# A decoder layer on one core: five of eight batches normed, and four routed to their experts, amid the last three attention rounds

## What is computed

```python
x1 = mixer(x)                                  # gated cumulative sums, a layer norm, a projection; then post-norm
q, k, v = x1 @ Wq, ctx @ Wk, ctx @ Wv          # 16 heads of 16
sm = softmax(einsum('nlhd,nshd->nlhs', q, k) / 4, axis=1)     # over the 512 queries
attn = einsum('nlhs,nshd->nlhd', sm, v).reshape(N, L, 256)
x2 = layernorm(x1 + attn @ Wo + bo)
logits = x2 @ Wr + br                          # 8 experts
top_idx = top_k(logits, 2)                     # two experts a token, softmax over the two logits
y = sum over the two experts of weight * (relu(x2 @ W1[e] + b1[e]) @ W2[e] + b2[e])
out = layernorm(x2 + y)
```

## Time and profile before

| what | value |
|---|---|
| median of three runs | 2198.38 us (2195.28 to 2202.76) |
| the profiled execution | 2195.98 us, of which 2194.3 us are the span of the profile |
| busy in the span | PE 90%, DVE 80%, ACT 70%, POOL 34% |
| last copy of attention outputs starts at | 1528.13 us |
| first matrix product of the experts at | 1647.92 us |

### The profile page before, as it was taken

One profiled execution on the slowest core, in us unless ns is written; L12 is line 12 of the kernel. 1 busy time (PEld: TensorE's weight loads), 2 busy tenths in 40 slices (PEclk: granted clock), 3 DMA queues, 4 the chain that ended last, 5 costly groups with the idle time before them and its releaser, 6 DMA issues.

```text
span 2194.3 us, 43516 instructions
## 1 busy us (share of the span) xinstructions
PE 1981.7 (90%) x10630; PEld 1044.8 (48%) x10638; DVE 1754.2 (80%) x3559; ACT 1540.5 (70%) x4345; POOL 736.3 (34%) x983
## 2 busy tenths in 40 slices
PE   7898998899999999999999998888829999999994
PEld 3554555322322232222322221112729999999994
DVE  5889885799999999999999999998635555555554
ACT  4655565899999999999999999998402333233333
POOL 0112111244444444444444441111563333333333
PEclk9989999999999999999999999999859999999997
DMA  4111105776758576676668576661771222222225
GB/s 156 44 44 72 58 24 130 193 125 116 112 110 145 118 110 117 119 124 135 90 131 136 108 111 92 123 77 42 223 197 32 37 36 37 36 36 36 36 36 168
DMA packets 126117, 212.39 MB, mean 97 GB/s; under 512 B 31554, under 2 KB 94786, under 8 KB 124882
## 3 DMA queue, kind: packets, MB, share of 16 engines
q1 hardware_dynamic: 98272, 151.74, 37.8%
q0 software_dynamic: 26240, 59.00, 10.2%
q10 hardware_dynamic: 1554, 1.05, 0.2%
HBM read 138.38 MB, written 73.74 MB: 97 GB/s over the span
## 4 chain that ended last, share of the span: by engine, by line
PE 39%; ACT 30%; issue 18%; DVE 7%; POOL 3%; DMA 2%; ACTq 1%; DVEq 0%; SPq 0%; POOLq 0%
ACT w_all L1429 26%; PE psum L1715 12%; PE psum L1725 11%; PE psum L473 6%; DVE neg_max L1336 3%; POOL list_all L1595 3%; PE psum L1239 2%; PE psum L1271 2%; ACT w_all L822 1%; PE psum L1702 1%; DMA v_all<-w_all 1%; PE psum L500 1%; ACTq L1428 1%; DVE stats L1016 0%; DVE stats L1995 0%
## 5 line engine op out<-in xcount | busy, mean ns | idle before, releaser
L1429 ACT ACTIVATE w_all<-psum,neg_max 128x512 f32<-128x512 f32 (+1 forms) x1664 | 1111.1, 736 | 18.2 <-DVE neg_max L1336 16.6
L1336 DVE TENSOR_REDUCE neg_max<-psum 128x1 f32<-128x512 f32 (+1 forms) x1664 | 1024.9, 677 | 17.3 <-PE psum L1271 14.2
L1271 PE MATMUL psum<-qst,kst 96*128 96x512 bf16 (+1 forms) x1664 | 527.7, 389 | 73.1 <-ACT w_all L1429 63.1
L1239 PE MATMUL psum<-w_all 128*32 128x512 f32 (+1 forms) x3328 | 448.9, 612 | 9.5 <-DVE w_all L1350 9.3
L1271 PEld LDWEIGHTS psum<-qst,kst 96*128 96x128 bf16 (+1 forms) x1664 | 130.0, 98 | 658.1 <-ACT w_all L1429 639.0
L1769 ACT ACTIVATE hid<-psum,b 128x128 f32<-128x128 f32 x568 | 161.9, 368 | 393.1 <-PE psum L1715 393.1
L1429 ACT ACTIVATION_READ_ACCUMULATOR w_all<-psum,neg_max 128x1 f32 (+1 forms) x1664 | 426.8, 257 | 0.0
L1402 POOL TENSOR_TENSOR w_all<-vst,inv 128x64 f32<-128x64 f32 (+1 forms) x416 | 121.0, 291 | 658.3 <-DVE inv L1304 654.7
L1715 PE MATMUL psum<-xst,w 128*128 128x128 f32 x2272 | 267.4, 277 | 0.0
L1715 PEld LDWEIGHTS psum<-xst,w 128*128 128x128 f32 x2272 | 261.6, 193 | 0.1
L1725 PE MATMUL psum<-area,hid 128*128 128x256 f32 x1136 | 257.0, 380 | 0.0
(11 more groups left out here) (209 smaller groups left out, 1878.1 us busy)
## 6 DMA issues: line engine op xcount, KB each, us to landing
kst<-k_parts SPq DMA_DIRECT2D x384, 112.0 KB, 6.5
k_parts<-k_out POOLq DMA_DIRECT2D x52, 336.0 KB, 3.0
w_all<-in_W SPq DMA_DIRECT2D x16, 1024.0 KB, 11.9
area<-in_ctxT SPq DMA_DIRECT2D x16, 896.0 KB, 4.7
vst<-v_all SPq DMA_DIRECT2D x64, 224.0 KB, 9.2
qst<-q_parts SPq DMA_DIRECT2D x192, 64.0 KB, 5.9
v_all<-area POOLq DMA_DIRECT2D x13, 896.0 KB, 4.3
q_parts<-q_out POOLq DMA_DIRECT2D x24, 256.0 KB, 3.0
```

The costliest lines, as they stand in the source:

```text
L1239: last = pe.matmul(psum[j * PAD:(j + 1) * PAD, 6, :], v_scaled[0:r, pb, j, :], probs_at[pb][0:r, j, :], start=t == 0, stop=t == ST - 1)
L1271: pe.matmul(psum[0:r, 2 * sbuf + i, :], kst[:, h, j, t * P:t * P + r], qst[:, h, j, :], start=True, stop=True).then_inc(scores_ready, 1)
L1336: v.tensor_reduce(neg_max[0:r, sbuf, i:i + 1], psum[0:r, 2 * sbuf + i], AX_X, ALU.min) \
L1429: act.activation(probs_at[pb][0:r, j, :], psum[0:r, 2 * sbuf + i, :], ACT.Exp, bias=neg_max[0:r, sbuf, i:i + 1], scale=-1.0, accum_out=sum ...
```

## The change

`NORMED_AT = (6, 13, 37, 44, 68)` names five steps among the 78 tile steps of the last three rounds. From each of them one batch (0 to 4) begins its norm, at fixed offsets: sums on PE in bank 7 at +0, +1, +3, +4 (`SUM_AT`), DVE's adds at +1 and +4, its statistics at +2 and +5, ACT's logarithm and exponential at +6 and +7, the shift on DVE and the scaling at +8 and +9. The scaling (`scale_rows`) is done by POOL here and not by ACT. Batches 0 to 3 (`PLACED`) are also turned (+13, +15, with ACT's copies in the same steps), scored and chosen (+17 to +20), given slots (+26 or +22) and scattered, one transfer a step from +27 or +28. The steps for batches 5 to 7, and the route of 4 to 7, stay in the route stage after attention.

The last three rounds are written out on every engine, where before two of them were in a loop on PE and DVE, and all three on ACT and POOL. The small tiles move into `xwk`, which is free after the last filled round. `y2`, `x2t` and `x2` move from the experts' own buffer `w1` to the places of the last three blocks of `w1_all` (`LATE_W1 = 3`), so that these three blocks are loaded only after the last `x2` is stored and scored. `y2` has two halves now. The table load that ACT had ahead of the route stage (`preload_act_table_set`) is gone.

```diff
+    NORMED_AT = (6, 13, 37, 44, 68)
+    NORMED, PLACED = len(NORMED_AT), len(NORMED_AT) - 1
...
+        LATE_W1 = 3
+        y2 = w1_all[:, E - 3].rearrange("p i (t d) -> p i t d", t=TT)
+        x2t = w1_all[:, E - 2, 0].rearrange("p (c l) -> p c l", c=C)
+        x2 = w1_all[:, E - 1].rearrange("p c (t d) -> p c t d", t=TT)
...
+            SUM_AT, ADD_AT, STATS_AT, TURN_AT = (0, 1, 3, 4), (1, 4), (2, 5), (13, 15)
+            LN_AT, ROOT_AT, SHIFT_AT, SCALE_AT = 6, 7, 8, 8
+            SCORE_AT, PAIR_AT, GAP_AT = 17, 18, 20
+            MASK_AT, RANK_AT, SCATTER_AT = (19, 20), (26, 22), (27, 28)
+            LOAD_AT, STORE_AT = 5, 11
...
+                half_round(B - 2, 0, 0, False)
+                for h in range(2):
+                    sp.wait_ge(attn_stored[h], 16 * GH * (FILLED - h) + OPEN)
+                store_heads(B - 2, 0, 1)
+                sp.wait_ge(items_ready, ITEMS * FILLED)
+                sp.wait_ge(v1_stored, 16 * FILLED)
+                for i in range(2):
+                    sp.wait_ge(k1_stored[i], 32 * FILLED)
+                load_route(sp, 0)
+                sp.dma_start(xwo, a["xWo"].rearrange("(c p) d -> p c d", p=P)).then_inc(xwo_loaded, 16)
+                load_route(sp, 1)
+                refill(B - 2, 0, 1, False)
...
+                def add_rows(b, i):
+                    if i == 0:
+                        wait(v, x2_ready, b - 1)
+                    v.wait_ge(proj_ready, 2 * b + i + 1)
+                    v.tensor_tensor(y2[:, b % 2, 2 * i:2 * i + 2].rearrange("p t d -> p (t d)"), psum[:, 7],
+                                    x1_in[:, b % 2, 2 * i:2 * i + 2].rearrange("p t d -> p (t d)"), ALU.add) \
+                        .then_inc(y2_ready, 1)
...
+                    if g is not None:
+                        route_step(g)
...
+                def scale_rows(b, ts):
+                    if ts[0] == 0:
+                        wait(pool, x2_stored[b % 2], 32 * (b // 2))
+                        wait(pool, x2t_ready, turned(b - 1))
+                        pool.wait_ge(rstd2_ready, b + 1)
+                        pool.wait_ge(shift2_ready, b + 1)
+                    for t in ts:
+                        last = pool.tensor_scalar(x2[:, b % 2, t], y2[:, b % 2, t], rstd2[:, t:t + 1], shift2[:, t:t + 1],
+                                                  ALU.mult, ALU.add)
...
+                def copy_turned(b, k):
+                    if k == 0:
+                        wait(act, logits_z_ready, b)
+                    act.wait_ge(x2t_ready, C * b + k + 1)
+                    act.activation(x2t[:, k], psum[:, 7], ACT.Copy).then_inc(x2t_copied, 1)
...
+                        if sub == 0 and g is not None:
+                            route_step(g)
...
-                for c in range(B):
+                for c in range(NORMED, B):
                     route_step(c)
                 for e in range(W2_EARLY, E):
                     load_w2(sp, e)
+                sp.wait_ge(logits_z_ready, B)
+                for h in range(2):
+                    sp.wait_ge(x2_stored[h], 16 * B)
+                for e in range(E - LATE_W1, E):
+                    load_weights(sp, e)
                 sp.dma_start(b2_all[:], a["b2"].rearrange("(o e) d -> o e d", o=1).to_broadcast([P, E, D])) \
                     .then_inc(b2_loaded, 16)
...
-                for e in range(B):
-                    scatter(e)
+                for b in range(PLACED, B):
+                    for at in range(2 * TT):
+                        scatter(pool, b, at)
...
-                act.preload_act_table_set("natural_log_exp_and_others")
-                for c in range(B + 1):
+                for c in range(NORMED, B + 1):
                     route_step(c)
```

More of the change, by code:

```diff
@@ new lines, in decoder_layer @@
+        stats2 = small([P, TT, 6])
+        moments2 = small([P, TT, 2])
+        rstd2_ln, rstd2, shift2 = (small([P, TT]) for _ in range(3))
+        mask = small([P, TT, E])
+        slot_at = small([P, TT + 1, E])
+        slot_of = small([P, TT, E])
+        slot_f = small([P, 2 * TT])
+        slot_u = small([P, B, 2 * TT], U32)
+        pairs = small([P, B, 2, TT, 2])
+        logits = small([P, TT, E])
+        top8 = small([P, TT, E])
+        top8_at = small([P, TT, E], U32)
+        chosen = small([P, TT, 2])
@@ new lines, in rank_masks, with root_of @@
+        def rank_masks(pe, b):
+            pe.wait_ge(mask_ready, b + 1)
+            wait(pe, slots_ready, b)
+            pe.matmul(psum[:, 7, 0:TT * E], before[:], mask.rearrange("p t e -> p (t e)"), start=True, stop=True)
+            pe.matmul(psum[:, 7, 64:64 + TT * E], ones[:], mask.rearrange("p t e -> p (t e)"),
+                      start=True, stop=True).then_inc(ranks_ready, 1)
+        def root_of(act, b):
+            act.wait_ge(moments2_ready, b + 1)
+            act.activation(rstd2_ln, moments2[:, :, 1], ACT.Ln, bias=eps_col[:]).then_inc(act_ln2, 1)
@@ L1272, in scores, with sum_rows @@
                                          qst[:, h, j, :], start=True, stop=True).then_inc(scores_ready, 1)
-                def tile_step(tile, it, fill):
+                def sum_rows(b, t):
+                    if t == 0:
+                        pe.wait_ge(route_loaded[b % 2], 32 * (b // 2 + 1))
+                        if b % 2 == 0:
+                            wait(pe, slots_ready, b)
+                    if b == 0 and t == 0:
+                        pe.wait_ge(xwo_loaded, 16)
+                        pe.wait_ge(items_read, ITEMS * FILLED + OPEN)
+                    if t % 2 == 0:
+                        wait(pe, y2_ready, 2 * b + t // 2)
+                    for k in range(C):
+                        last = pe.matmul(psum[:, 7, t % 2 * D:(t % 2 + 1) * D], at_in[:, b % 2, k, t * P:(t + 1) * P],
+                                         xwo[:, k, :], start=k == 0, stop=k == C - 1)
+                    if t % 2 == 1:
+                        last.then_inc(proj_ready, 1)
@@ new lines, in turn_rows @@
+                def turn_rows(b, k):
+                    if k == 0:
+                        pe.wait_ge(x2_ready, b + 1)
+                        if b % 2 == 0:
+                            pe.wait_ge(y2_ready, 2 * (b + 2))
+                        else:
+                            pe.wait_ge(logits_ready, b)
+                    else:
+                        pe.wait_ge(x2t_copied, C * b + k)
+                    for t in range(TT):
+                        last = pe.transpose(psum[:, 7, t * P:(t + 1) * P], x2[:, b % 2, t, k * P:(k + 1) * P],
+                                            ident[:])
+                    last.then_inc(x2t_ready, 1)
@@ L1433, in decoder_layer @@
+                with act.Fori(0, FILLED) as it:
+                    for tile in range(N_TILE):
+                        tile_step(tile, it, None)
+                for g in range(LAST_STEPS):
+                    it, tile = divmod(g, N_TILE)
+                    tile_step(tile, FILLED + it, g)
+                for g in range(LAST_STEPS, LAST_STEPS + LAG):
+                    route_step(g)
         heads_ctx.close()
```

549 lines of the change are left out of this document (318 added, 231 removed).

## The result

| | before | changed |
|---|---|---|
| median of 12 executions each, us | 2200.02 (2195.28 to 2203.22) | 2193.68 (2190.43 to 2199.23) |
| span of the profiled execution, us | 2194.3 | 2191.3 |
| ratio to before, 95% interval | | 0.9976 (0.9965 to 0.9986) |
| first copy of the written-out rounds to the last (the **stretch**) | 204.1 | 233.7 |
| last copy (A) to the first expert matmul | 119.8 | 87.5 |

The kernel became 0.24% faster by the ratio, where I had forecast 0.6% (2198.4 to 2186). By the bound set in the prediction that is no change: 6.3 us between the medians, 3.0 between the spans. Both large terms came, with the signs expected, but attention paid 29.6 us and not 22, and the route stage gave 32.3 and not 34.5.

A forecast was written before the change was run, and what follows sets the result against it. ACT bounds unfilled attention rounds (2.67 us a tile), DVE close behind; in the route stage scatters and weight loads end nearly together. Attention +22, route stage -34.5, sum -12.5 us: 2198.4 to 2186, range 2172 to 2204.

The forecast's parts named there:

- the bound set in the prediction: Whole kernel: a measurement can tell about 0.3%, 6.6 us, from no change.
- DVE becomes the bound: Attention, last three rounds: DVE's added 32 us make it the bound, and ACT's added 8.2 us hide in its waits.
- 8 a round, below the 14.2 that a filled round takes in: Attention: PE's added 24 us over three rounds fit, since filled rounds take 14.2 us of extra matmuls and grow by 0.8.
- the slack of 11.5 us: Attention: DVE's added work of 32 us was forecast to lengthen the last three rounds by only 20.5.
- My test: Attention: DVE's summed work, 70.4 us, predicts a filled round's measured 70.17 within 0.3 us.
- Rival 3: Attention pays for DVE and ACT: bursts empty score banks, ACT's copies come on top; +34 to +40, 2201 us, chance 0.13.
- the main case: Forecast as written: attention +22 us, route stage -34.5, time 2186 us; 2178 to 2194 has chance 0.54.
- Rival 2: Attention hides more: DVE's small operations fit in gaps, ACT stays the bound; +8 to +12, 2174 us, chance 0.10.
- rival 4: Attention: loads of heads queue behind route transfers on SP, four each 6 us late, 24 us more; 2210 us, chance 0.09.
- POOL's result is needed only three steps (8 us) later: Attention: POOL's 20 scalings and 32 scatters cost nothing; if that cover failed, 41 us in all.
- rival 5: Route stage: batch 4's slots come late, so the scatters' chain isn't shortened; a 4 us stall hidden behind weights, no chance given.
- my average of 8.6 a batch: Route stage before: the seven batches after the first took 60.5 us to the last `x2` store, 8.6 each.

The follow-up runs named there:

- before_look: The kernel before, unchanged, profiled a second time: 2199.1 us, stretch 204.2 us, 121.9 us from A to the first expert matmul.
- one_normed: Changed kernel with only one batch normed amid attention (from step 68) and none routed: median 2224.1 us, ratio to before 1.0021, stretch 207.3 us.

## Why the prediction was wrong by half

**What bounds the kernel: right.** The prices per insert were right within 11%, DVE was the engine with the largest sum, and the route stage had two chains that end together.

**The step that failed** is "DVE becomes the bound. ACT's 8.2 then lies in the time in which it waits for DVE", and with it PE's "8 a round, below the 14.2 that a filled round takes in" and the slack of 11.5 us (32 less 20.5) that the sum gave back in full. It compared sums of whole rounds. My test, that a filled round takes DVE's sum within 0.3 us, holds for eleven inserts of 0.4 to 0.65 us on DVE in 26 steps; it says nothing on bursts of three engines in different steps. What the runs showed in its place: 3.8 us added to ACT cost 4.6, 14.6 added to PE cost 7.3, and 7.1 us of stalls stand at seven steps, where I had put 1.5. By terms:

| term of attention | forecast | measured |
|---|---|---|
| DVE's inserts | +32 | +29.7 |
| slack used up | -11.5 | -8.5 |
| new stalls at single steps (late load, turns, copies, scores) | +1.5 | +7.1 |
| end of the last round, behind POOL | 0 | +1.4 |
| sum | +22 | +29.6 |

Rival 3 had the mechanism of the third line (the turn on PE queues behind scores, and ACT's copies come on top), at +34 to +40; the truth lies between it and the main case. I had given it 0.13. Rival 2 is refuted, and rival 4 was there with 0 to 4.7 us and not 24. "POOL's result is needed only three steps (8 us) later" was right but for the end of the last round, which has no step behind it.

**Route stage: nearly right.** Per term: last `x2` store at A + 29.4, forecast 26.5. PE waited there for batch 7's second load, and DVE's slots of batch 4, ahead of batch 6's `x2`, for the counts that stood behind it on PE:

```profile
1572.73 3.20 PE L1967 MATMUL psum<-area 128*128 128x256 f32 x8 [3.30 <-DMA area<-x_all]
```

```profile
1576.66 0.75 DVE L316 TENSOR_TENSOR xwk<-xwk,psum 128x8 f32<-128x8 f32 x4 [4.97 <-PE psum L250]
```

This is rival 5, which I had called hidden behind the weights. It is not: the weights start behind the same chain. The kernel before has the same wait once (3.45 us) among its seven steps from store to store, so my average of 8.6 a batch spread it thin: the changed kernel's two steps took 12.5 and 7.1. From the store to the bias's landing 50.8, forecast 40.1 + 10.5 = 50.6. From the landing to the first matmul 7.3, forecast 8.3: the lists, issued 8.6 us before the bias had landed, reached DVE 0.2 us after it. That agrees with the rule that I had weighed from the Trainium skill (DMA: Bandwidth & Descriptors, Queues, rings and completion order), that descriptors are consumed in ring order; before, a list load on an idle queue took 1.7 us.

**Time.** -2.0 us at the first expert matmul: 0.8 later at the first copy, +29.6, -32.3. The expert stage gave 1.0 more. The forecast missed by 7.6 + 2.2 us, and only the first is clear of the scatter between executions. A net of two terms of 20 to 35 has little left when one of them is off by a third. The range (2172 to 2204) held; the chance of 0.72 for faster by over 0.3% did not reckon with that.

## What to carry to other kernels

When engines pass work on every few microseconds and two of them are within a tenth of the bound, don't hide an insert by comparing sums over a round: lay it on the step in which it stands, for each engine, and give it only the slack of that step. Read the length of a step from an operation that comes once in each. And where a stage ends in a queue of loads, ask of every load when its place comes free: moving 8 MB forward gave 8 to 13 us (2186.0 and 2181.1, beside 2194), where the whole change had given 6 to 7.

## What the runs showed of the hardware

- The kernel before took 2200 us on some chips and 2219 on two others, the changed one 2192 to 2194 wherever it ran, one of those two included. The kernel before was not profiled there (`before_look` was to do it, but met a chip on which it takes 2199), so the cause is open. A kernel with seven batches in the route stage, run on one of those two, has stretches in it in which PE, DVE and ACT stand together. Waits of DVE in the route stage of `one_normed`, and a window of it:

```profile
DVE xwk L279 <- remote: 28.0, 3, 15.1
```

```profile
1560.00:1570.00 10.00, 1.25 (x5) 1.15 (x6) 3.37 (x20) 1.23 (x2) 4.79 (x5) 0.61 0.03 1
```

  DMA moved 1 GB/s in it, so in this window no transfer of the program is what they wait for. The longest wait (15.1 us, until 1608.2) had 113 to 131 GB/s beside it at first and 1 GB/s only in its last 5.2 us. The change moves most of this stage into attention, which may be why it is worth 1.2% there and 0.3% elsewhere; that is argued, not shown.
- The landing of scatters depends on what else is queued: the lists, which wait for it, went 11.3 us after the last scatter with weights in the queues at 227 GB/s, and 6.6 with most of them landed, at 136. The two profiles of the kernel before lie along it: 7.3 us at 134 GB/s and 9.7 at 165. The Trainium skill (DMA: Bandwidth & Descriptors, Queues, rings and completion order) says that a semaphore increment lands only after every earlier write of the same DMA engine, across its queues, which would bring this about; the runs show the size only.
- The scores of one batch (16 matmuls of eight columns in the trace, with a 128x128 f32 weight load each) took 1.85 us in all four places amid attention. In `one_normed`'s route stage they took 1.85 to 1.93 us five times and 3.55 or 3.56 three times; the granted clock was 1.00 in the five windows and 0.50 in the three. Over whole rounds the granted clock was 0.92 and 0.93 in the last two, against 0.98 and 0.97 before.
